# A table gather with a small network behind it: the late tiles' share of the totals goes from SBUF sums to PSUM, and TensorE's order in the last stage changes

## The chip, the core and the metric

One core of a Trainium2 chip. Times are device microseconds of one execution, the median of several runs; lower is better. The engines are TensorE (PE in the profile, its weight loads PEld), VectorE (DVE), ScalarE (ACT), GpSimd (POOL) and SyncE (SP, which here only issues DMAs). SBUF is the working memory, PSUM the memory that TensorE writes, here eight banks of 128 partitions by 512 float32.

## What is computed

For B = 512 samples, 26 tables of 6250 rows by D = 128 and 13 numerical inputs, all float32, the reference computes:

```python
emb = jax.vmap(lambda tab, idx: tab[idx])(tables, cat_features)      # 26 x 512 x 128
emb_btd = jnp.transpose(emb, (1, 0, 2))
wide_num = relu(numerical @ w_wide + b_wide)
cat_sum = jnp.sum(emb_btd, axis=1)                                   # 512 x 128
linear_output = cat_sum + wide_num
x = jnp.concatenate([numerical, emb_btd.reshape(512, 26 * 128)], axis=1)
x = relu(x @ W1 + b1)                                                # 512 x 256
x = relu(x @ W2 + b2)                                                # 512 x 128
dnn_output = x @ W3 + b3                                             # 512 x 1
return sigmoid(dnn_output + linear_output)                           # 512 x 128
```

So every gathered row is used twice: in the first layer, and in the sum over the tables (the total).

## The kernel before

The samples are four chunks of 128 (CH = 4). A tile is the 128 rows of one table for one chunk; a gather brings it with the samples on the partitions, TensorE turns (transposes) it into PSUM, an engine copies it to SBUF, and TensorE multiplies it with that table's slice of W1 into the first layer's four banks. The sums over the tables are held turned, in `emb_sum` in SBUF.

**The body** (L392 to L403) goes through 46 parts of two tiles each (LAST = 46). For each part TensorE turns both tiles (`turn_part`, L336) and multiplies them by W1 (`sum_part`, L353, two products of 256 columns); DVE copies the turned part (L546) and adds it to `emb_sum` (L553). Table 12 is picked by one-hot products instead (L362), with its picture in the two `total` banks, which the body so occupies. Tiles of table 0 of chunks 1 to 3 are fetched row by row with DMAs that ACT and SP issue (L256).

**The last stage** works on the late tables 23 and 24: eight tiles, n = 0 to 7, tile n belonging to chunk n // 2. Each is turned into one of the two `turn` banks (`turn_tile`, L405, L412), copied to `late_t` by ACT (`copy_tile`, L631, L633), multiplied by W1 (`sum_tile`, L415, L421: two products of 128 columns) and, in the kernel before, added from its turned picture to `emb_sum` by DVE (`add_tile`, L580, L587). When a chunk has both tiles, ACT takes the lower half of its first layer through relu (L637) and DVE the upper half (L572); `layer2` (L433, L436) gives the second layer, DVE takes it through relu (`relu_h2`, L575, L577), and `layer3` (L440, L444) adds its product with W3, spread over all 128 columns, to the chunk's total in the bank `total[c % 2]`. Ahead of that `begin_total` (L426, L431) has turned the chunk's `emb_sum` back into that bank by a product with the identity. ACT squashes the total by a sigmoid (`squash`, L640, L642) and SP stores it (L283).

Every product of 128 columns in float32 stands in the profile as two loads and two matmuls, so `sum_tile` and `layer2` are four of each, `begin_total` and `layer3` two, and a turn is one.

The order of each engine's work is written out by hand, and each engine goes through it strictly in that order, waiting on semaphores. TensorE's is in L449 to L468 (printed below). DVE's is in L589 to L598: for each chunk its first add, the upper relu of the chunk before, the second add, and for chunks 1 and 2 the second layer's relu of the chunk before. ACT's is in L647 to L656: copy of the chunk's first tile, lower relu of the chunk before, squash of two chunks before, copy of the second tile. ACT's order is not touched by the change.

In the text behind, turn 4 is `turn_tile(4)`, product 4 is `sum_tile(4)`, and so on, with chunks as well: layer3(0) is the call for chunk 0.

Of the kernel before, what the change touches and what calls it, by code (L numbers as in the profile page):

```python
# [25 lines left out]
def build(nc, num, cat, tables, w_wide, b_wide, W1, b1, W2, b2, W3, b3, out):  # L26
# [58 lines left out]
    with ctx:  # L85
# [6 lines left out]
        def sem(name):  # L92
            return ctx.enter_context(nc.semaphore(name))
# [4 lines left out]
        def late_turn(n):  # L98
            return turn[(LAST + n) % 2][:, 0:P]
# [9 lines left out]
            return first_layer[0][c % 2][:, HW + c // 2 * P:HW + (c // 2 + 1) * P]  # L109

        def total_of(c):
            return total[c % 2][:, 0:D]

        def by_halves(ap):
            return ap.rearrange("x (j q p) -> x q j p", j=HALF, q=2)
# [1 line left out]
        def sum_chunk(c):  # L117
            return emb_sum[:, c % 2, chunk(c // 2)]
# [102 lines left out]
        used = sem("used")  # L221

        late_gathered = [sem(f"late_gathered{n}") for n in range(TILES)]
        late_turned = sem("late_turned")
        late_copied = sem("late_copied")
        late_added = sem("late_added")
# [90 lines left out]
        def _(pe):  # L317
# [35 lines left out]
            def sum_part(i):  # L353
                t, q = PARTS[i]
                wait_w1(t)
                pe.wait_ge(copied, i + 1)
                for k in range(KH):
                    mm = nc.tensor.matmul(first_half(k, q), w1[:, t, chunk(k)], emb_t[:, i % SLOTS, :],  # L358
                                          start=False, stop=False, skip_group_check=True)
                mm.then_inc(used, 1)  # L360
# [44 lines left out]
            def turn_tile(n):  # L405
                c, g = divmod(n, LATE)
                pe.wait_ge(late_gathered[n], 16)
                if n < 2:
                    pe.wait_ge(added, LAST - 1 + n)
                else:  # L410
                    pe.wait_ge(late_added, n - 1)
                nc.tensor.transpose(late_turn(n), emb[:, LATE_TABLES[g], c, :], ident[:, :]  # L412
                                    ).then_inc(late_turned, 1)

            def sum_tile(n):  # L415
                c, g = divmod(n, LATE)
                pe.wait_ge(late_copied, n + 1)
                if c >= 2:
                    pe.wait_ge(h2_ready, c - 1)
                for k, done in enumerate([h1_low_done, h1_high_done]):  # L420
                    mm = nc.tensor.matmul(first_chunk(k, c), w1[:, LATE_TABLES[g], chunk(k)], late_t[:, n, :],  # L421
                                          start=False, stop=False, skip_group_check=True)
                    if g == LATE - 1:
                        mm.then_inc(done, 1)

            def begin_total(c):  # L426

                pe.wait_ge(late_added, (c + 1) * LATE)
                if c >= 2:
                    pe.wait_ge(y_ready, c - 1)  # L430
                nc.tensor.matmul(total_of(c), sum_chunk(c), ident[:, :], start=True, stop=False, skip_group_check=True)  # L431

            def layer2(c):  # L433
                for k, ready in enumerate([h1_low_ready, h1_high_ready]):
# [4 lines left out]

            def layer3(c):  # L440
                pe.wait_ge(h2_ready, c + 1)
                if c == 0:
                    pe.wait_ge(w3_ready, 1)
                nc.tensor.matmul(total_of(c), h2[:, chunk(c)], w3_wide[:, :],  # L444
                                 start=False, stop=True, skip_group_check=True).then_inc(final_done, 1)
# [3 lines left out]
            for c in range(CH):  # L449
                n = c * LATE  # L450
                turn_tile(n)
                if c == 0:
                    sum_part(LAST - 1)
                else:
                    sum_tile(n - 1)
                    begin_total(c - 1)
                if c >= 2:
                    layer3(c - 2)
                turn_tile(n + 1)
                sum_tile(n)  # L460
                if 1 <= c < CH - 1:
                    layer2(c - 1)
            sum_tile(TILES - 1)
            layer2(CH - 2)
            layer2(CH - 1)
            layer3(CH - 2)
            begin_total(CH - 1)
            layer3(CH - 1)  # L468

        @block.vector  # L470
        def _(dve):
# [103 lines left out]
            def relu_h2(c):  # L575
                dve.wait_ge(h2_done, c + 1)
                nc.vector.tensor_scalar(h2[:, chunk(c)], second_chunk(c), b2_col, 0.0, ALU.add, ALU.max  # L577
                                        ).then_inc(h2_ready, 1)

            def add_tile(n):  # L580
                c, g = divmod(n, LATE)
                dve.wait_ge(late_copied, n + 1)
                if n == 0:
                    dve.wait_ge(added, LAST)
                else:
                    dve.wait_ge(late_added, n)
                nc.vector.tensor_tensor(sum_chunk(c), late_turn(n), sum_chunk(c), ALU.add).then_inc(late_added, 1)  # L587

            for c in range(CH):  # L589
                add_tile(c * LATE)  # L590
                if c >= 1:
                    relu_h1_high(c - 1)
                add_tile(c * LATE + 1)
                if 1 <= c < CH - 1:
                    relu_h2(c - 1)
            relu_h1_high(CH - 1)
            relu_h2(CH - 2)
            relu_h2(CH - 1)  # L598

        @block.scalar  # L600
# [79 lines left out]
```

## Time and profile before

| | us |
|---|---|
| median of 3 runs | 236.08 (235.92 to 236.24) |
| time of the profiled execution | 237.66 |
| its span, first to last instruction | 235.9 |
| TensorE busy, matmuls | 126.2 |
| DVE busy | 76.9 |
| ACT busy | 6.2 |
| GpSimd busy | 93.1 |
| mean granted TensorE clock | 0.841 of full |

The profile shows one execution. Its time, 237.66 us, is 1.58 us above the median of the runs beside it, and its span is 0.2 us below that median. Busy times overlap between engines; what counts is who waits for whom at each point. The chain of waits starts from the last instruction and goes back to what released each step. A timeline lists instructions in order of time with start and length; a bracket gives the idle time of that engine just before and what ended it. Lines of like instructions in a row are merged (x4).

### The profile page before, as it was taken

The numbers are of one execution on the slowest core, as the hardware profiler recorded it, in microseconds if no ns is written. First come the engines' busy times: TensorE is split into PE (matmuls) and PEld (weight loads), VectorE is DVE, ScalarE is ACT, GpSimd is POOL, SyncE is SP. The second block draws the span as 40 slices with busy tenths as digits, with TensorE's granted clock in tenths as the row PEclk, the third lists the DMA queues.
The fourth block names the chain that finished last, engine by engine and source line by source line (L and its number), as shares of the span: only waits on it lengthen the run. The fifth ranks groups of instructions, "written<-read, shape, count | busy, mean of one in ns | idle before, by whom it ended". The sixth has DMA issues, their size and how long they took to land.

```text
span 235.9 us, 2252 instructions
## 1 busy us (share of the span) xinstructions
PE 126.2 (54%) x476; PEld 82.6 (35%) x476; DVE 76.9 (33%) x182; ACT 6.2 (3%) x18; POOL 93.1 (39%) x106
## 2 busy tenths in 40 slices
PE   2638200059000700060002719999999999999695
PEld 0415100034000300030002206666666666667594
DVE  3150000033000200110003018677667666845352
ACT  0200000000000000000000000000000000000052
POOL 5777777777777777777771000000000000000000
PEclk9999999999855555575555667999999999999999
DMA  5997613565545443362422003400000000000001
GB/s 150 331 262 170 106 47 51 52 47 103 54 61 45 103 57 48 52 97 54 52 54 63 5 2 93 138 9 4 4 5 4 2 2 1 2 6 2 1 13 34
DMA packets 11244, 14.06 MB, mean 60 GB/s; under 512 B 3308, under 2 KB 8015, under 8 KB 11231
## 3 DMA queue, kind: packets, MB, share of 16 engines
q0 software_dynamic: 3104, 6.36, 20.7%
q1 hardware_dynamic: 4768, 3.80, 5.4%
q10 hardware_dynamic: 3359, 3.76, 5.2%
q8 instruction: 4, 0.07, 0.1%
q14 instruction: 9, 0.07, 0.1%
HBM read 13.65 MB, written 0.26 MB: 59 GB/s over the span
## 4 chain that ended last, share of the span: by engine, by line
SPq 57%; issue 34%; PE 5%; DMA 1%; DVE 1%; ACT 0%; DVEq 0%
SPq L256 50%; SPq L251 7%; PE first_layer L358 1%; PE first_layer L421 1%; DMA first_cat<-in_r_cat_features 1%; PE first_layer L436 1%; PE total L444 1%; DMA emb<-in_L_rec_tables 0%; PE total L431 0%; PE turn L412 0%; PE turn L344 0%; ACT y L642 0%; PE total L320 0%; DVE row_idx L503 0%; DVE cat_row L495 0%
## 5 line engine op out<-in xcount | busy, mean ns | idle before, releaser
L299 POOL DMA_INDIRECT emb<-in_L_rec_tables,row_idx x95 | 89.7, 944 | 29.0 <-issue 29.0
L358 PE MATMUL first_layer<-emb_t,w 128*128 128x256 f32 x184 | 54.4, 423 | 68.2 <-issue 61.3
L358 PEld LDWEIGHTS first_layer<-emb_t,w 128*128 128x128 f32 x184 | 37.6, 212 | 94.4 <-issue 81.8
L369 PE MATMUL total<-hot,block_rows 128*128 128x512 f32 (+1 forms) x98 | 53.8, 656 | 24.8 <-issue 24.8
L546 DVE COPY emb_t<-turn 128x256 f32<-128x256 f32 x46 | 19.4, 422 | 105.4 <-remote 78.3
L526 DVE TENSOR_SCALAR hot<-total,row_no 128x512 f32<-128x512 f32 x49 | 35.3, 742 | 0.0
L369 PEld LDWEIGHTS total<-hot,block_rows 128*128 128x128 f32 (+1 forms) x98 | 17.5, 211 | 32.0 <-issue 32.0
L344 PE MATMUL turn<-ident,emb 128*128 128x128 f32 x92 | 20.3, 304 | 9.0 <-DMA emb<-in_L_rec_tables,row_idx 5.5
L344 PEld LDWEIGHTS turn<-ident,emb 128*128 128x128 f32 x92 | 13.9, 156 | 16.3 <-DMA emb<-in_L_rec_tables,row_idx 6.6
L553 DVE TENSOR_TENSOR emb_sum<-turn,emb_sum 128x256 f32<-128x256 f32 x44 | 18.3, 415 | 0.0
L533 DVE TENSOR_SCALAR wide<-total,b_sb 128x4 f32<-128x4 f32 x1 | 0.2, 222 | 31.6 <-issue 31.6
L633 ACT COPY late_t<-turn 128x128 f32<-128x128 f32 x8 | 2.1, 264 | 219.2 <-PE turn L412 219.2
L421 PE MATMUL first_layer<-late_t,w 128*128 128x128 f32 x32 | 5.0, 280 | 0.1
L421 PEld LDWEIGHTS first_layer<-late_t,w 128*128 128x128 f32 x32 | 4.2, 191 | 0.4 <-ACT late_t L633 0.2
L334 PE MATMUL first_layer<-num_t,w_num 13*128 13x256 f32 x8 | 3.8, 649 | 0.8 <-DVE num_t L509 0.8
L587 DVE TENSOR_TENSOR emb_sum<-turn,emb_sum 128x128 f32<-128x128 f32 x8 | 2.3, 292 | 3.0 <-ACT late_t L633 2.9
L334 PEld LDWEIGHTS first_layer<-num_t,w_num 13*128 13x128 f32 x8 | 2.5, 325 | 1.8 <-DVE num_t L509 1.3
L513 DVE TENSOR_SCALAR pick_lim<-pick_cat 128x512 f32<-128x512 int32 x1 | 0.4, 427 | 7.6 <-DMA pick_cat<-in_r_cat_features 7.6
L320 PE MATMUL total<-ident,cat_row 104*128 104x104 f32 x1 | 0.4, 408 | 4.0 <-DVE cat_row L495 4.0
L436 PE MATMUL first_layer<-h,w 128*128 128x128 f32 x16 | 2.3, 278 | 0.0
L412 PE MATMUL turn<-ident,emb 128*128 128x128 f32 x8 | 2.2, 272 | 0.0
L436 PEld LDWEIGHTS first_layer<-h,w 128*128 128x128 f32 x16 | 2.1, 191 | 0.0
(54 smaller groups left out, 34.2 us busy)
## 6 DMA issues: line engine op xcount, KB each, us to landing
emb<-in_L_rec_tables SPq DMA_DIRECT2D x256, 0.5 KB
block_rows<-in_L_rec_tables ACTq DMA_DIRECT2D x12, 256.0 KB, 2.9
w<-in_L_rec_W SPq DMA_DIRECT2D x2, 1152.0 KB
emb<-in_L_rec_tables ACTq DMA_DIRECT2D x128, 0.5 KB
emb<-in_L_rec_tables,row_idx POOLq DMA_INDIRECT x95
w<-in_L_rec_W SPq DMA_DIRECT2D x1, 768.0 KB
w<-in_L_rec_W SPq DMA_DIRECT2D x1, 256.0 KB
pick_cat<-in_r_cat_features ACTq DMA_DIRECT2D x1, 256.0 KB
```

Source lines behind the costliest of these rows:

```text
L251: eng.load(regs, cat_byte[t * CH + c:t * CH + c + 1, lo:lo + REGS])
L256: eng.dma_start(emb[b:b + 1, t, c, :].bitcast(U8), row_bytes[t:t + 1, bass.ds(at, ROW)]).then_inc(fetched[t, c], 16)
L299: nc.gpsimd.indirect_dma_start(emb[:, t, c, :], None, rows, bass.IndirectOffsetOnAxis(ap=index, axis=0)).then_inc(landed, 16)
L334: nc.tensor.matmul(first_half(k, q), w1_num[:, chunk(k)], cols, start=True, stop=True)
L344: mm = nc.tensor.transpose(turn[i % 2][:, chunk(j)], emb[:, t, c, :], ident[:, :])
L358: mm = nc.tensor.matmul(first_half(k, q), w1[:, t, chunk(k)], emb_t[:, i % SLOTS, :], start=False, stop=False, skip_group_check=True)
L369: mm = nc.tensor.matmul(pick_bank[:, :], block_rows[0:n, j, :], hot[0:n, j % PICK_RING, :], start=(j == 0), stop=(j == PER))
L421: mm = nc.tensor.matmul(first_chunk(k, c), w1[:, LATE_TABLES[g], chunk(k)], late_t[:, n, :], start=False, stop=False, skip_group_check=True)
L436: mm = nc.tensor.matmul(second_chunk(c), w2[:, k, :], h1[:, k, chunk(c)], start=False, stop=False, skip_group_check=True)
L526: nc.vector.tensor_scalar(hot[:, j % PICK_RING, :], pick_row[:, :], row_no[:, j:j + 1], None, ALU.is_equal).then_inc(hot_ready, 1)
L546: nc.vector.tensor_copy(emb_t[:, i % SLOTS, :], turn[i % 2][:, 0:HW]).then_inc(copied, 1)
L553: nc.vector.tensor_tensor(emb_sum[:, q, :], turn[i % 2][:, 0:HW], emb_sum[:, q, :], ALU.add).then_inc(added, 1)
```

## The change

- `total_of(c)`: the four totals get places of their own, two in each `total` bank, where before chunks c and c + 2 shared the first 128 columns of one bank.
- `begin_totals` replaces the four calls of `begin_total`: the `emb_sum` of all four chunks, as the body leaves them, are turned into the totals one after the other, right behind the last part's products.
- `add_tile` on DVE takes the gathered tile as it lies in SBUF, not its turned picture, and adds it to the total in PSUM. It waits for `begin_totals`, for its gather, for the add before, and for chunks 2 and 3 for the squash of the chunk that shares the bank. It no longer waits for ACT's copy.
- `turn_tile` waits for ACT's copy out of the `turn` bank instead of DVE's add; `layer3` waits for the chunk's adds.
- TensorE's order: from chunk 1 on the products of the previous chunk's second tile and of this chunk's first come together, ahead of this chunk's second turn; `layer3(c - 2)` stands right behind the chunk's first turn; `layer2(CH - 2)` comes ahead of the last product.
- DVE's order: the upper relu ahead of both adds, the second layer's relu behind them, for all chunks.

```diff
--- before.py
+++ after.py
@@ -109,7 +109,7 @@
             return first_layer[0][c % 2][:, HW + c // 2 * P:HW + (c // 2 + 1) * P]
 
         def total_of(c):
-            return total[c % 2][:, 0:D]
+            return total[c % 2][:, c // 2 * D:(c // 2 + 1) * D]
 
         def by_halves(ap):
             return ap.rearrange("x (j q p) -> x q j p", j=HALF, q=2)
@@ -221,6 +221,7 @@
         used = sem("used")
 
         late_gathered = [sem(f"late_gathered{n}") for n in range(TILES)]
+        totals_begun = sem("totals_begun")
         late_turned = sem("late_turned")
         late_copied = sem("late_copied")
         late_added = sem("late_added")
@@ -408,7 +409,7 @@
                 if n < 2:
                     pe.wait_ge(added, LAST - 1 + n)
                 else:
-                    pe.wait_ge(late_added, n - 1)
+                    pe.wait_ge(late_copied, n - 1)
                 nc.tensor.transpose(late_turn(n), emb[:, LATE_TABLES[g], c, :], ident[:, :]
                                     ).then_inc(late_turned, 1)
 
@@ -423,12 +424,14 @@
                     if g == LATE - 1:
                         mm.then_inc(done, 1)
 
-            def begin_total(c):
-
-                pe.wait_ge(late_added, (c + 1) * LATE)
-                if c >= 2:
-                    pe.wait_ge(y_ready, c - 1)
-                nc.tensor.matmul(total_of(c), sum_chunk(c), ident[:, :], start=True, stop=False, skip_group_check=True)
+            def begin_totals():
+
+
+                pe.wait_ge(added, LAST)
+                for c in range(CH):
+                    mm = nc.tensor.matmul(total_of(c), sum_chunk(c), ident[:, :], start=(c < 2), stop=False,
+                                          skip_group_check=True)
+                mm.then_inc(totals_begun, 1)
 
             def layer2(c):
                 for k, ready in enumerate([h1_low_ready, h1_high_ready]):
@@ -439,6 +442,7 @@
 
             def layer3(c):
                 pe.wait_ge(h2_ready, c + 1)
+                pe.wait_ge(late_added, (c + 1) * LATE)
                 if c == 0:
                     pe.wait_ge(w3_ready, 1)
                 nc.tensor.matmul(total_of(c), h2[:, chunk(c)], w3_wide[:, :],
@@ -451,20 +455,18 @@
                 turn_tile(n)
                 if c == 0:
                     sum_part(LAST - 1)
+                    begin_totals()
                 else:
+                    if c >= 2:
+                        layer3(c - 2)
                     sum_tile(n - 1)
-                    begin_total(c - 1)
-                if c >= 2:
-                    layer3(c - 2)
+                sum_tile(n)
                 turn_tile(n + 1)
-                sum_tile(n)
-                if 1 <= c < CH - 1:
+                if c >= 1:
                     layer2(c - 1)
             sum_tile(TILES - 1)
-            layer2(CH - 2)
             layer2(CH - 1)
             layer3(CH - 2)
-            begin_total(CH - 1)
             layer3(CH - 1)
 
         @block.vector
@@ -578,23 +580,25 @@
                                         ).then_inc(h2_ready, 1)
 
             def add_tile(n):
+
                 c, g = divmod(n, LATE)
-                dve.wait_ge(late_copied, n + 1)
-                if n == 0:
-                    dve.wait_ge(added, LAST)
-                else:
+                dve.wait_ge(totals_begun, 1)
+                if c >= 2:
+                    dve.wait_ge(y_ready, c - 1)
+                if n > 0:
                     dve.wait_ge(late_added, n)
-                nc.vector.tensor_tensor(sum_chunk(c), late_turn(n), sum_chunk(c), ALU.add).then_inc(late_added, 1)
+                dve.wait_ge(late_gathered[n], 16)
+                nc.vector.tensor_tensor(total_of(c), total_of(c), emb[:, LATE_TABLES[g], c, :], ALU.add
+                                        ).then_inc(late_added, 1)
 
             for c in range(CH):
-                add_tile(c * LATE)
                 if c >= 1:
                     relu_h1_high(c - 1)
+                add_tile(c * LATE)
                 add_tile(c * LATE + 1)
-                if 1 <= c < CH - 1:
+                if c >= 1:
                     relu_h2(c - 1)
             relu_h1_high(CH - 1)
-            relu_h2(CH - 2)
             relu_h2(CH - 1)
 
         @block.scalar
```

## Rows read from the trace of the kernel before

**Rows 1.** The page: shares of the span on the chain that ended last, by engine.

```profile
SPq 57%; issue 34%; PE 5%; DMA 1%; DVE 1%; ACT 0%; DVEq 0%
```

**Rows 2.** Windows: from:to, length, busy (x instructions) per engine, granted clock, DMA share, GB/s.

```profile
218.00:220.40 2.40, 0.00 (x0) 0.00 (x0) 0.00 (x0) 0.00 (x0) 0.00 (x0) 1.00 0.01 2
223.45:230.55 7.10, 7.10 (x60) 6.83 (x58) 3.85 (x13) 3.43 (x13) 0.00 (x0) 1.00 0.04 11
```

**Rows 3.** Timeline, TensorE's weight loads: start, us, engine, line, operation, count [idle <-releaser].

```profile
220.47 0.14 PEld L344 LDWEIGHTS turn<-ident,emb 128*128 128x128 f32 x1 [2.85 <-DMA emb<-in_L_rec_tables]
...
223.67 0.73 PEld L358 LDWEIGHTS first_layer<-emb_t,w 128*128 128x128 f32 x4
224.65 0.53 PEld L421 LDWEIGHTS first_layer<-late_t,w 128*128 128x128 f32 x4
```

**Rows 4.** The same timeline, from layer2(1) to the last turn.

```profile
228.49 0.53 PEld L436 LDWEIGHTS first_layer<-h,w 128*128 128x128 f32 x4
228.94 0.14 PEld L412 LDWEIGHTS turn<-ident,emb 128*128 128x128 f32 x1
229.05 0.53 PEld L421 LDWEIGHTS first_layer<-late_t,w 128*128 128x128 f32 x4
229.50 0.30 PEld L431 LDWEIGHTS total<-ident,emb_sum 128*128 128x128 f32 x2
229.72 0.30 PEld L444 LDWEIGHTS total<-w_wide,h 128*128 128x128 f32 x2
229.94 0.14 PEld L412 LDWEIGHTS turn<-ident,emb 128*128 128x128 f32 x1
```

**Rows 5.** The same timeline, from the last product to the last instruction.

```profile
230.83 0.52 PEld L421 LDWEIGHTS first_layer<-late_t,w 128*128 128x128 f32 x4 [0.25 <-ACT late_t L633]
231.27 1.03 PEld L436 LDWEIGHTS first_layer<-h,w 128*128 128x128 f32 x8
232.43 0.30 PEld L444 LDWEIGHTS total<-w_wide,h 128*128 128x128 f32 x2
232.65 0.30 PEld L431 LDWEIGHTS total<-ident,emb_sum 128*128 128x128 f32 x2
232.93 0.30 PEld L444 LDWEIGHTS total<-w_wide,h 128*128 128x128 f32 x2
```

**Rows 6.** Timeline of ACT in the last stage.

```profile
229.36 0.27 ACT L633 COPY late_t<-turn 128x128 f32<-128x128 f32 x1 [0.59 <-PE turn L412]
229.58 0.37 ACT L637 ACTIVATE h<-first_layer,vec_cols 128x128 f32<-128x128 f32 x1
230.25 0.37 ACT L642 ACTIVATE y<-total,wide 128x128 f32<-128x128 f32 x1 [0.30 <-PE total L444]
230.52 0.26 ACT L633 COPY late_t<-turn 128x128 f32<-128x128 f32 x1
...
232.96 0.87 ACT L642 ACTIVATE y<-total,wide 128x128 f32<-128x128 f32 x2 [1.24 <-PE total L444]
```

**Rows 7.** Timeline of DVE in the last stage.

```profile
229.25 0.35 DVE L577 TENSOR_SCALAR h<-first_layer,vec_cols 128x128 f32<-128x128 f32 x1 [0.16 <-PE first_layer L436]
229.66 0.29 DVE L587 TENSOR_TENSOR emb_sum<-turn,emb_sum 128x128 f32<-128x128 f32 x1
229.87 0.34 DVE L572 TENSOR_SCALAR h<-first_layer,vec_cols 128x128 f32<-128x128 f32 x1
...
231.58 0.35 DVE L572 TENSOR_SCALAR h<-first_layer,vec_cols 128x128 f32<-128x128 f32 x1 [0.48 <-PE first_layer L421]
232.03 0.85 DVE L577 TENSOR_SCALAR h<-first_layer,vec_cols 128x128 f32<-128x128 f32 x2
```

**Rows 8.** Timeline of DVE near the start, two dependent operations, the second writing PSUM.

```profile
14.65 0.43 DVE L516 TENSOR_SCALAR pick_neg<-pick_lim 128x512 f32<-128x512 f32 x1
15.11 0.70 DVE L519 TENSOR_TENSOR total<-pick_neg,pick_lim 128x512 f32<-128x512 f32 x1
```

**Rows 9.** Timeline of TensorE's weight loads in the body, at granted clock 0.50.

```profile
77.42 1.35 PEld L358 LDWEIGHTS first_layer<-emb_t,w 128*128 128x128 f32 x4 [19.55 <-issue]
```

## Prediction

> **What bounds the kernel now.** I read the chain of waits first. Most of it is SP's queue [rows 1]: the row-by-row fetches, whose last landing releases TensorE at 220.47 after an idle stretch [rows 3]. The change touches nothing ahead of that, nor the body's last parts behind it, so a gain or loss can only arise from 223.5 us on. For that stretch I read the windows and then the timelines. In the windows the reader is to see that TensorE has no idle time between 223.45 and 230.55 (7.10 busy of 7.10), while DVE is busy for 3.85 and ACT for 3.43, and that the clock is full [rows 2]. TensorE's throughput is the limit there. The engines beside it have slack, but their hand-overs don't hurt only because the order of TensorE's work puts enough between a producer and its user. From 230.83 on it is otherwise: TensorE waits for other engines, and a chain of latencies leads to the end [rows 5].
>
> **The prices.** I count in slots, the starts of the weight loads. Product or layer2: 228.49 to 228.94, 0.45. Turn: 0.11. begin_total or layer3: 0.22 [rows 4]. Hand-overs, from a load's start:
> - Turn to product by ACT's copy: load 228.94 [rows 4], copy 229.36 for 0.27 [rows 6]; the copy of 230.52 ends at 230.78 and the product starts at 230.83 [rows 5, 6], 0.05 on. Sum 0.74.
> - layer2 to layer3 by DVE's relu: load 228.49 [rows 4], relu 229.25 for 0.35 [rows 7]; the relu of 232.03 ends at 232.38 and layer3 starts at 232.43 [rows 5, 7]. Sum 0.76 + 0.35 + 0.05 = 1.16.
> - Product to layer2's upper half: load 230.83, relu 231.58 for 0.35, again 0.05: 1.15 [rows 5, 7].
> - Product to ACT's lower relu: 229.05 to 229.58, 0.53. layer3 to squash: 229.72 to 230.25, 0.53 [rows 4, 6]. ACT's next operation starts 0.27 after a squash has started (230.25, 230.52), DVE's 0.21 after an add (229.66, 229.87) [rows 6, 7].
>
> **The parts of the change.**
>
> *The begins.* Same four, same 0.22 each. Three lay between other TensorE work and one, begin_total(3), between layer3(2) and layer3(3): 232.65 to 232.87 [rows 5]. There it filled a hole: the relu that layer3(3) needs ends at 0.85 after 232.03, that is 232.88, and layer3(3) starts at 232.93 [rows 5, 7]. Taking it away from the end gains nothing, and putting it at the start costs its 0.22 in a stretch where TensorE is full.
>
> *layer2(2) ahead of the last product.* It stood behind it, beside the wait for the relus of chunk 3, which is idle time otherwise. Moving it delays the last product by 0.45, less the wait that it covers.
>
> *The copy and the turns.* The last body products start at 223.67 and product 0 at 224.65, with one turn before it [rows 3], so the begins start at 224.54 and last 0.89, to 225.43. Product 0 then runs to 225.87 and turns 1 and 2 take until 226.09. Product 1 comes next, but its copy needs 225.87 + 0.74 = 226.61. **First stall: 0.52.** Before, product 0 stood between turn 1 and turn 2.
>
> *layer3 behind the turn.* Products 1 and 2 go to 227.50, turn 3 to 227.61, layer2(0) starts at 227.61 (its upper half, from 227.83, has its relu since 226.61 + 1.15 = 227.76) and ends at 228.05. Turn 4 ends at 228.16, and layer3(0) follows at once, though its relu needs 227.61 + 1.16 = 228.77. **Second stall: 0.61.** Behind the waiting layer3 stand products 3 and 4, which need nothing of it. Before, a product and a begin (0.67) stood here [rows 4]; they hid exactly this. Chunk 3 repeats it: products 3 and 4 from 228.99, turn 5 at 229.88, layer2(1) at 229.99, turn 6 from 230.43 to 230.54, layer3(1) at 229.99 + 1.16 = 231.15. **Third stall: 0.61.**
>
> *The adds, and DVE's new wait.* Eight adds read SBUF instead of a turned picture and write PSUM. No row shows that form: 0.29 for the old form [rows 7] is one bound, 0.70 for an add of four times the columns that writes PSUM [rows 8] the other; nothing excludes slightly less than 0.29, which would change nothing. I take 0.29, since the size is the same and the 0.70 is for 512 columns. Adds 0 to 3 lie in DVE's idle time. Add 4 waits for squash(0), and the relu of chunk 1's second layer is queued behind it; layer3(1) waits for that. squash(0) follows the lower relu of chunk 1: 228.99 + 0.53 = 229.52, squash from 229.79 to 230.16. With the 0.03 between dependent operations (14.65 + 0.43 to 15.11) [rows 8], adds 4 and 5 start at 230.19 and 230.51, and DVE can start the relu 0.21 later, at 230.72. It is due at 229.99 + 0.76 = 230.75. So the detour by the squash just fits, cost 0; at 0.70 an add it would cost 0.8. ACT has no queue ahead of any copy that counts.
>
> *The end.* layer3(1) at 231.15, products 5 and 6 to 232.26, turn 7 to 232.37, layer2(2) to 232.82, and product 7 at 232.26 + 0.74 = 233.00. **Fourth stall: 0.18.** From the last product to layer3(3) it was 232.93 - 230.83 = 2.10 [rows 5], all by hand-overs: 1.15 to layer2(3)'s upper half, a relu, layer3. Nothing in that is changed, and squash and store behind it are as before.
>
> **The sum.** The last product moves from 230.83 to 233.00: **+2.17**. As a check by parts: work moved ahead of it, 0.22 + 0.45 = 0.67; new stalls 0.52 + 0.61 + 0.61 + 0.18 = 1.92; less the 0.34 that it waited before (turn 7 at 229.94, two steps of 0.11 and 0.45 to 230.50, start at 230.83 [rows 4, 5]) and some 0.06 lost around turn 2. That is 2.19, the same within rounding. The profiled span would be 235.9 + 2.2 = 238.1, its time 237.66 + 2.17 = 239.8. The median lies 1.58 below the profiled time, and I carry that over: 236.08 + 2.17 = 238.25, say **238.2**.
>
> A rule that speaks for smaller stalls: by the Trainium skill (TensorE: Matmul & The Clock Gate, Part 2, Step-by-step) TensorE can pull weight loads ahead of matmuls in flight, though matmuls keep their order. By it one load (two that overlap take 0.30 [rows 5], so under 0.2) might be done within each wait and the four stalls would shrink to a sum of about 1.2, for some 237.5. The trace speaks against it for this wait: the load of product 7 began only at 230.83, after the copy [rows 5], though W1 had long been there.
>
> **Rivals.**
> - *Only throughput counts.* If the hand-overs were met (an order of waits that I misread, or relus and copies that come sooner once DVE no longer waits for the copy), only the 0.67 moved ahead of the last product remains, less the 0.34 + 0.06 of old waits: +0.27, 236.35. For it speaks that TensorE was full for 7.1 us without one wait [rows 2]. Against it: a turn and its product now stand 0.11 apart, where the row has 0.74. This is the case that is not slower.
> - *A gain.* If begin_total(3) were on the path at the end rather than in a hole, and the hand-overs met, the 0.22 comes off: 235.86. Against it stand the 232.88 and 232.93 above. A gain of over 0.2% needs twice that, from something that I don't see.
> - *DVE becomes the bound.* With an add of 0.70, from any price above about 0.32 on, the squash, add, add, relu detour decides chunk 3: layer3(1) 0.8 later; then adds 6 and 7 and a relu (some 1.8) stand in front of the upper relu of chunk 3, from squash(1) on, and cost about another 0.8. Total +3.8, 239.9.
> - *The clock falls in the gaps.* TensorE would have three gaps of over 0.5 us in 7. At the lower clock four loads of 256-column products took 1.35 [rows 9] against 0.73 [rows 3]. Some 25 slots behind the third stall would then cost up to 0.11 more each, but half lie beside waits: +1.4 more, 239.6. Against it: the 2.40 us without any work at 218 left the clock at full [rows 2]. The Trainium skill (TensorE: Matmul & The Clock Gate, Part 1: The HAM clock gate) has it that an idle TensorE is put back to half its clock; the trace agrees for much longer gaps only.
>
> **How the numbers follow.** Forecast with stalls at row prices: 0.82. Only throughput: 0.06. A gain or no change by something unseen: 0.04. DVE as the bound: 0.05. Clock: 0.03. The forecast's own range: each of the four stalls can be off by 0.15 either way if hand-overs vary, the adds can cost up to 0.4 before they reach the rival, and the runs before spread by 0.3: 237.5 to 238.9. With the other cases left out that holds about 8 in 10. A measurement of this kernel can tell 0.2%, 0.47 us, from no change. Faster: 0.03. Within 0.2%: 0.07, the throughput case and part of the unseen. Slower: 0.90.
>
> **What would show it.** In TensorE's timeline behind the begins: idle time before product 1 ended by ACT's copy, before layer3(0) and layer3(1) by DVE's relu L577, about 0.5 to 0.6 each, and a small one before product 7. The begins 0.89 in a row without idle time. DVE's add 0.29. The last product to the last layer3 2.10 as before. TensorE idle for less than 1 us between 223.5 and the last product would prove the throughput case; layer3(1) released by a relu that itself stood behind an add, the DVE case. The prediction is wrong as a whole if the body itself ends at another time than 223.5.

## The result and the profile after

The changed kernel takes 239.03 us in the median of 5 runs (238.05 to 239.89) against 236.08 (235.84 to 236.35) before: slower, ratio 1.0119, 95% interval 1.0087 to 1.0151. A second comparison gave a ratio of 1.0107 (1.0084 to 1.0129), 238.58 against 236.43. The forecast was 238.2, with a range of 237.5 to 238.9: the 239.03 lies 0.13 us above that range, the 238.58 in it.

| | before, first profile | after, first profile |
|---|---|---|
| span | 235.9 | 237.2 |
| last fetched row releases TensorE | 220.47 | 219.49 |
| turn 0 | 223.45 | 222.48 |
| last product (product 7) | 230.83 | 232.20 |
| layer3(3) | 232.93 | 234.30 |
| turn 0 to last product | 7.38 | 9.72 |
| last product to layer3(3) | 2.10 | 2.10 |

All starts are those of the weight loads. The late stage, counted from turn 0 so that the body's end doesn't matter, grew by 2.34 us. The last fetched row happened to release TensorE 0.98 earlier in this profile than in that of before, and the body ended as much earlier.

TensorE's weight loads of the changed kernel, from turn 0 on (start, us, line, operation, count, idle time before and what ended it), beside [rows 3 to 5]:

```profile
222.48 0.14 PEld L413 LDWEIGHTS turn<-ident,emb 128*128 128x128 f32 x1
222.69 0.73 PEld L359 LDWEIGHTS first_layer<-emb_t,w 128*128 128x128 f32 x4
223.45 1.08 PEld L432 LDWEIGHTS total<-ident,emb_sum 128*128 128x128 f32 x8
224.45 0.53 PEld L422 LDWEIGHTS first_layer<-late_t,w 128*128 128x128 f32 x4
224.89 0.25 PEld L413 LDWEIGHTS turn<-ident,emb 128*128 128x128 f32 x2
225.63 0.97 PEld L422 LDWEIGHTS first_layer<-late_t,w 128*128 128x128 f32 x8 [0.48 <-ACT late_t L637]
...
227.78 0.30 PEld L448 LDWEIGHTS total<-w_wide,h 128*128 128x128 f32 x2 [0.57 <-DVE h L579]
...
230.35 0.30 PEld L448 LDWEIGHTS total<-w_wide,h 128*128 128x128 f32 x2 [0.76 <-DVE h L579]
...
231.57 0.53 PEld L439 LDWEIGHTS first_layer<-h,w 128*128 128x128 f32 x4
232.20 0.52 PEld L422 LDWEIGHTS first_layer<-late_t,w 128*128 128x128 f32 x4
```

The reader is to see three brackets where [rows 4] has none: TensorE waits for ACT's copy before product 1, and for DVE's relu before each of the first two layer3. (The idle time of the loads is counted from the end of the last one, so a stall in slots, the starts of the loads, is a little longer: 0.52, 0.60 and 0.79.) The fourth stall has no bracket: layer2(2) starts at 231.57 and would end at 232.02, and product 7 starts 0.18 later.

The same stretch as a window (from:to, length, busy time of each engine, granted clock):

```profile
222.48:232.20 9.72, 8.62 (x66) 7.63 (x65) 3.96 (x13) 3.64 (x13) 0.00 (x0) 1.00 0.03 8
```

TensorE had no idle time at all in [rows 2] (and 0.06 us up to the last product); now it has 1.10 us of it, and the clock stays full. The four stalls add up to 2.09 us in slots, since the matmuls of the loads before a stall still run into it.

### The profile page after: what moved, and what is told of

Read it like the earlier page. It is cut to its first block, busy times and chain, and to the rows that moved or that the text cites. A ratio compares the mean times of both kernels' runs of the same rounds, so it can differ in the third digit from the quotient of the medians.

```text
span 237.2 us, 2257 instructions
## 1 busy us (share of the span) xinstructions
PE 125.3 (53%) x476; PEld 81.7 (34%) x476; DVE 77.2 (33%) x182; ACT 6.2 (3%) x18; POOL 93.0 (39%) x106
## 4 chain that ended last, share of the span: by engine, by line
SPq 59%; issue 33%; PE 5%; ACT 1%; DVE 1%; DMA 1%; DVEq 0%
SPq L257 51%; SPq L252 7%; PE first_layer L359 1%; PE first_layer L422 1%; SPq L270 1%; PE first_layer L439 1%; PE total L448 1%; DMA emb<-in_L_rec_tables 1%; DVE h L579 0%; PE total L432 0%; PE turn L345 0%; ACT h L641 0%; ACT y L646 0%; DVE total L591 0%; PE turn L413 0%
## 5 line engine op out<-in xcount | busy, mean ns | idle before, releaser
L370 PE MATMUL total<-hot,block_rows 128*128 128x512 f32 (+1 forms) x98 | 53.2, 649 | 27.4 <-issue 27.4
L345 PE MATMUL turn<-ident,emb 128*128 128x128 f32 x92 | 20.0, 301 | 8.0 <-DMA emb<-in_L_rec_tables,row_idx 6.2
L591 DVE TENSOR_TENSOR total<-total,emb 128x128 f32<-128x128 f32 x8 | 2.4, 298 | 2.8 <-PE total L432 2.0
L448 PE MATMUL total<-w_wide,h 128*128 128x128 f32 x8 | 1.9, 313 | 1.1 <-DVE h L579 1.1
L574 DVE TENSOR_SCALAR h<-first_layer,vec_cols 128x128 f32<-128x128 f32 x4 | 1.4, 350 | 3.1 <-PE first_layer L422 3.0
```

The costliest lines, as they stand in the source:

```text
L345: mm = nc.tensor.transpose(turn[i % 2][:, chunk(j)], emb[:, t, c, :], ident[:, :])
L370: mm = nc.tensor.matmul(pick_bank[:, :], block_rows[0:n, j, :], hot[0:n, j % PICK_RING, :], start=(j == 0), stop=(j == PER))
```

## The experiments

Two things were in question: which part of the change costs, TensorE's order or the new totals; and why the medians differ by more than the 2.34 us of the late stage. Late stage below means turn 0 to the last product; where an expectation counts from the turn that the last row releases, it is 2.98 us more while the clock stays full.

### The two kernels again

> The kernel before, once more. The late stretch, from the turn that the last fetched row releases to the last product's first load, should be 10.4 us as in its first profile, whatever the body does. Theory 1 (what the late stage doesn't explain of the 2.95 us between the medians, some 0.6 us, is the body ending at a varying time): the moment at which the last row releases TensorE differs by some tenths up to 1.5 us from profile to profile of the same kernel. Theory 2 (the change moves the body): that moment is within 0.2 us in all profiles of the kernel before, and later in all of the changed one.

> The changed kernel, once more. The late stretch should be 12.7 us as in its first profile. Theory 1 (the body's end varies by itself): the ratio to the kernel before comes nearer to 1.010, the 2.35 us of the late stretch alone. Theory 2 (the change moves the body): the ratio stays near 1.0119.

The kernel before had 236.05 us beside 236.43 for the same code (ratio 0.9999, 0.9973 to 1.0025), the changed one the 1.0107 told above. Two weight loads of the kernel before in this profile, the turn released by the last row and the last product:

```profile
219.15 0.14 PEld L344 LDWEIGHTS turn<-ident,emb 128*128 128x128 f32 x1 [0.90 <-DMA emb<-in_L_rec_tables]
...
229.51 0.52 PEld L421 LDWEIGHTS first_layer<-late_t,w 128*128 128x128 f32 x4 [0.25 <-ACT late_t L633]
```

From one to the other it is 10.36 us, as in the first profile (220.47 to 230.83); the changed kernel again had 12.71 (218.86 to 231.57). The late stage repeats to 0.01 us. The moment at which the last row releases TensorE does not: 220.47, 219.15 and, in a third profile below, 220.39 with the old code; 219.49 and 218.86 with the new; 219.32 to 220.48 in four variants below that leave the body alone. So nothing shows the change moving the body later, and its own cost is 2.35 us, 1.0100, which lies in both intervals. The medians differ by 2.95 us in the first comparison and by 2.15 in the second, once above and once below that. The variation of the body is large enough for both; which executions had it was not traced.

### The new totals alone, and the new order alone

The changed kernel with the old order of TensorE's calls:

```diff
                 if c == 0:
                     sum_part(LAST - 1)
                     begin_totals()
                 else:
-                    if c >= 2:
-                        layer3(c - 2)
                     sum_tile(n - 1)
-                sum_tile(n)
+                if c >= 2:
+                    layer3(c - 2)
                 turn_tile(n + 1)
-                if c >= 1:
+                sum_tile(n)
+                if 1 <= c < CH - 1:
                     layer2(c - 1)
             sum_tile(TILES - 1)
+            layer2(CH - 2)
             layer2(CH - 1)
```

> Begins in front and DVE's adds to the totals as in the changed kernel, but TensorE's order of turns, products, layer2 and layer3 as before. Theory (the order costs): the stall before product 1 shrinks to 0.1 and those before layer3 to 0.16 and 0.3; the last product comes 0.55 us later than before, late stretch 10.9 us, time about 236.7. Rival (the early begins and the adds with their wait for the squash cost): late stretch over 12.3 us, time about 238.5.

The late stage took 8.06 us (222.31 to 230.37), 0.69 more than before and 1.67 less than the changed kernel: near the theory, far from the rival. Yet the time was 237.46, ratio 1.0045 (1.0029 to 1.0061), because something that I had not expected was late next. TensorE's load of layer2(3)'s upper half, then DVE's timeline:

```profile
230.37 0.52 PEld L422 LDWEIGHTS first_layer<-late_t,w 128*128 128x128 f32 x4 [0.25 <-ACT late_t L638]
...
232.23 0.30 PEld L439 LDWEIGHTS first_layer<-h,w 128*128 128x128 f32 x2 [0.62 <-DVE h L575]
```

```profile
231.57 0.35 DVE L580 TENSOR_SCALAR h<-first_layer,vec_cols 128x128 f32<-128x128 f32 x1 [0.52 <-PE first_layer L439]
231.84 0.34 DVE L575 TENSOR_SCALAR h<-first_layer,vec_cols 128x128 f32<-128x128 f32 x1
```

With layer2(2) back behind the last product, DVE's new order has chunk 2's second relu (231.57) in front of chunk 3's upper relu. The latter was due at 230.37 + 0.75 = 231.12 and started at 231.84; the end grew from 2.10 to 2.80 us. The two halves of the change were made for each other: DVE's order needs layer2(2) ahead of the last product.

The kernel before with the new order of TensorE's calls, its begins put behind the chunk's products:

```diff
                 if c == 0:
                     sum_part(LAST - 1)
                 else:
+                    if c >= 2:
+                        layer3(c - 2)
                     sum_tile(n - 1)
+                sum_tile(n)
+                if c >= 1:
                     begin_total(c - 1)
-                if c >= 2:
-                    layer3(c - 2)
                 turn_tile(n + 1)
-                sum_tile(n)
-                if 1 <= c < CH - 1:
+                if c >= 1:
                     layer2(c - 1)
             sum_tile(TILES - 1)
-            layer2(CH - 2)
             layer2(CH - 1)
```

> The kernel before with the changed TensorE order alone: both products ahead of a chunk's second turn, layer3 right behind the first turn, layer2(2) ahead of the last product; sums, begins (now behind the chunk's products) and adds as before. Theory (the order costs): stalls of 0.5 before product 1, 0.6 before layer3(0) and layer3(1), 0.2 before product 7; late stretch 12.3 us, time about 238.1. Rival (the new totals cost): late stretch at most 10.8 us, time about 236.3.

```profile
224.57 0.97 PEld L421 LDWEIGHTS first_layer<-late_t,w 128*128 128x128 f32 x8 [0.48 <-ACT late_t L633]
...
227.01 0.30 PEld L444 LDWEIGHTS total<-w_wide,h 128*128 128x128 f32 x2 [0.62 <-DVE h L577]
...
229.66 0.30 PEld L444 LDWEIGHTS total<-w_wide,h 128*128 128x128 f32 x2 [0.62 <-DVE h L577]
...
231.73 0.52 PEld L421 LDWEIGHTS first_layer<-late_t,w 128*128 128x128 f32 x4
```

These weight loads show the changed kernel's stalls in the old data path. The late stage was 9.42 us, the time 238.69, ratio 1.0105 (1.0084 to 1.0126), which can't be told from the changed kernel's 238.58. Order alone costs 2.05 us of late stage, the new totals alone 0.69 with a late end; the change 2.35. With the new order in place, the new totals add only 0.30: 0.22 for the begin that came from the end, and 0.08 at the two layer3, whose stalls in slots are 0.66 and 0.65 here and 0.60 and 0.79 in the changed kernel. The order is the cause of most of it.

### The stalls one by one

The next four ran on a chip that gives the kernel before 133.95 us, of which below. Their late stages are read in the same way and set beside the 9.72 us of the changed kernel, which was not itself profiled on that chip. What supports it is that the stalls which an experiment leaves alone are as long there (before product 1 an idle time of 0.48, before layer3(0) 0.57).

```diff
                     relu_h1_high(c - 1)
+                if c == 2:
+                    relu_h2(c - 1)
                 add_tile(c * LATE)
                 add_tile(c * LATE + 1)
-                if c >= 1:
+                if c >= 1 and c != 2:
                     relu_h2(c - 1)
```

> The changed kernel with one step of DVE's order moved: the second layer's relu of chunk 1 goes ahead of adds 4 and 5. Theory (layer3(1)'s stall of 0.79 is 0.61 of plain hand-over and 0.18 of the detour squash, add, add): that stall falls to 0.6, the others stay, late stretch 12.5 us instead of 12.7. Rival (0.79 is the hand-over itself, longer in the second layer3 than in the first for another reason): late stretch unchanged at 12.7.

```profile
126.56 0.30 PEld L448 LDWEIGHTS total<-w_wide,h 128*128 128x128 f32 x2 [0.57 <-DVE h L579]
```

The second layer3 now waits as long as the first (0.57 idle instead of 0.76), late stage 9.53 instead of 9.72: theory. The plain hand-over is 0.6, the detour by the squash 0.19.

```diff
-                sum_tile(n)
-                turn_tile(n + 1)
+                if c == 0:
+                    turn_tile(n + 1)
+                    sum_tile(n)
+                else:
+                    sum_tile(n)
+                    turn_tile(n + 1)
```

> The changed kernel with turn 1 ahead of product 0 instead of behind it. Theory (product 1's stall of 0.5 is the missing distance between turn and product): the stall falls to 0.1, late stretch 12.3 us, time 0.4 us less than the changed kernel's. Rival (the gap only moves on, since layer3(0) waits for a relu whose time is set elsewhere): late stretch 12.6 to 12.7.

```profile
121.35 0.14 PEld L413 LDWEIGHTS turn<-ident,emb 128*128 128x128 f32 x1
121.53 1.08 PEld L422 LDWEIGHTS first_layer<-late_t,w 128*128 128x128 f32 x8
```

Product 1 starts 0.18 behind turn 2's start, 0.07 of it stall. Late stage 9.39, a gain of 0.33 where 0.4 was expected: the eight loads take 1.08 instead of 0.97, since product 2 follows its own turn too closely as well and waits 0.1 for its copy.

```diff
                 else:
+                    sum_tile(n - 1)
                     if c >= 2:
                         layer3(c - 2)
-                    sum_tile(n - 1)
                 sum_tile(n)
```

> The changed kernel with layer3(c - 2) behind the first product of a chunk instead of ahead of it. Theory (the two stalls before layer3 come from nothing being left between layer2 and layer3): they fall from 0.60 and 0.79 to 0.16 and 0.3, and the last product comes 0.9 us earlier, late stretch 11.8 us, time about 237.6. Rival (DVE, with its adds behind the squash, sets the pace of a chunk, so that TensorE's order doesn't matter): the second stall stays above 0.7 and the late stretch above 12.3.

```profile
125.97 0.30 PEld L448 LDWEIGHTS total<-w_wide,h 128*128 128x128 f32 x2 [0.17 <-DVE h L579]
...
127.37 0.52 PEld L422 LDWEIGHTS first_layer<-late_t,w 128*128 128x128 f32 x4
```

The long waits are gone, only 0.17 idle is left at layer3(1); late stage 8.80 us, 0.92 less than the changed kernel, as worked out. Moving layer3 past one product gives back 0.9 of the 2.35 us. Its ratio to the kernel before there was 1.0048 (1.0026 to 1.0070), against 1.0093, 1.0080 and 1.0100 for the other three on this chip.

```diff
                 dve.wait_ge(totals_begun, 1)
-                if c >= 2:
-                    dve.wait_ge(y_ready, c - 1)
-                if n > 0:
-                    dve.wait_ge(late_added, n)
                 dve.wait_ge(late_gathered[n], 16)
+                if c >= 2 and n % LATE == 0:
+                    dve.wait_ge(late_added, n)
+                    dve.wait_ge(y_ready, c - 1)
+                elif n > 0:
+                    dve.wait_ge(late_added, n)
```

> The changed kernel with the order of the adds' waits changed alone: those long satisfied (the gather, the begins) first, the one that is released last (the squash for adds 4 and 6, the add before for the others) last. Theory (each wait that stands behind the last released one costs DVE's queue 0.05 to 0.1 us on the chain, twice behind the squash and the first add): add 5 starts 0.35 after add 4 instead of 0.50, layer3(1)'s stall falls from 0.79 to about 0.63, late stretch 12.55. Rival (the 0.50 is the latency of one add to a dependent one in PSUM): nothing changes, 12.7.

First the chain of waits of the changed kernel between squash(0) and layer3(1), in order of time; then that of this experiment, from the same squash to add 5:

```profile
228.90 0.27 ACT y L646
229.17 0.03 DVEq L590
229.20 0.05 issue
229.25 0.31 DVE total L591
229.56 0.03 issue
229.59 0.02 DVEq L589
229.61 0.05 issue
229.66 0.05 DVEq L590
229.71 0.04 issue
229.75 0.30 DVE total L591
230.05 0.26 DVE h L579
```

```profile
125.45 0.03 issue
125.48 0.05 DVEq L589
125.53 0.04 issue
125.58 0.31 DVE total L592
125.89 0.03 issue
125.91 0.05 DVEq L591
125.96 0.04 issue
126.01 0.30 DVE total L592
```

The expectation was missed: late stage 9.70, a gain of 0.02. Add 5 does start sooner behind add 4 (0.43 instead of 0.50), so the 0.50 is not the latency of an add in PSUM. But the edit also took the wait for the squash out of add 5, which leaves it three waits instead of four, and the number may count more than the order: in the changed kernel's first profile add 1, with three waits in the old order, followed add 0 by 0.39 (224.76, 225.15). The two were not tested apart. And add 4 now starts 0.14 behind the squash's end instead of 0.08, and the gain is gone. From the squash's end it is 0.03 and 0.05 to the add in the one, 0.03, 0.05 and 0.04 in the other; why the second takes longer was not found.

### The new totals at their best

The first experiment's order of TensorE, with DVE's mended:

```diff
                     relu_h1_high(c - 1)
+                if c == 2:
+                    relu_h2(c - 1)
                 add_tile(c * LATE)
                 add_tile(c * LATE + 1)
-                if c >= 1:
+                if c == 1:
                     relu_h2(c - 1)
             relu_h1_high(CH - 1)
+            relu_h2(CH - 2)
```

> The begins in front and the adds to the totals kept, in the best order I know for them: TensorE's turns, products and layers as in the kernel before, the relu of chunk 1's second layer ahead of adds 4 and 5, the upper relu of chunk 3 ahead of the second layer's relu of chunk 2. Theory (the new totals save nothing, since the adds and the last begin lay in slack, and cost 0.2 at the start and some waits at layer3): turn 0 to the last product 7.95 us, the end 2.1 again, 0.6 us slower than before on a chip at 236 us. Rival (the new totals are worth something once the order is mended): under 7.4 us, no slower than before.

```profile
230.68 0.52 PEld L422 LDWEIGHTS first_layer<-late_t,w 128*128 128x128 f32 x4 [0.23 <-ACT late_t L641]
...
232.78 0.30 PEld L448 LDWEIGHTS total<-w_wide,h 128*128 128x128 f32 x2 [0.20 <-DVE h L580]
```

Turn 0 was at 222.77, so the late stage is 7.91 us and the end 2.10: 0.53 more than before in all. The time, 237.07 against 236.81, ratio 1.0006 (0.9984 to 1.0027), can't tell that from nothing; its interval reaches 0.64 us. What the trace does tell is that the new totals, freed of the changed order, bring no gain in the best order that I know for them.

### The kernel before again, and two that beat it

> The kernel before, a third time. Two chips so far gave it 236 and 134 us, with the same instructions. Theory: on the chip at 134 us the gathers, one each 1.25 us to about 124.6, come so late that turns of the late stage wait for them, so that from turn 0 to the last product it takes about 8.5 us instead of 7.4 and the changed order has less to lose (0.6 to 1.4 us instead of 2.4). On a chip at 236 us: 7.4 us again, all gathers landed at 140. Rival: 7.4 us on both kinds of chip.

This run was on a chip at 236 us, so the expectation's first half was not put to the test; the late stage was 7.37 us once more. But this profile (237.5 us of span) shows one thing that makes the body's end vary. The window and the weight loads behind the wait for the last row:

```profile
220.40:224.00 3.60, 3.60 (x11) 2.90 (x12) 1.51 (x4) 0.00 (x0) 0.00 (x0) 0.55 0.00 0
```

```profile
220.39 0.14 PEld L344 LDWEIGHTS turn<-ident,emb 128*128 128x128 f32 x1 [2.34 <-DMA emb<-in_L_rec_tables]
220.40 1.18 PEld L358 LDWEIGHTS first_layer<-emb_t,w 128*128 128x128 f32 x4
...
225.06 0.14 PEld L412 LDWEIGHTS turn<-ident,emb 128*128 128x128 f32 x1
```

Behind an idle stretch of 2.34 us the granted clock was near half for 3.6 us, and from the released turn to turn 0 it took 4.67 us instead of 2.98. With 239.26 us this execution was the slowest of its 14.

The kernel before with turn 7 and product 6 ahead of layer3(1), and ACT's copy of tile 7 ahead of the squash of chunk 1:

```diff
-                if c >= 2:
+                if c == 2:
                     layer3(c - 2)
                 turn_tile(n + 1)
                 sum_tile(n)
+                if c == 3:
+                    layer3(c - 2)
...
-                if c >= 2:
+                if c == 2:
                     squash(c - 2)
                 copy_tile(c * LATE + 1)
             relu_h1_low(CH - 1)
+            squash(CH - 3)
```

> The kernel before with one thing mended: turn 7 and product 6 ahead of layer3(1), and ACT's copy of tile 7 ahead of the squash of chunk 1, which goes behind the lower relu of chunk 3. Theory: product 7 no longer waits 0.33 for a copy that stood behind a squash; turn 0 to the last product falls from 7.38 to 7.05 us, the end behind it stays 2.10, time 0.3 us less on a chip at 236 us; on one at 134 us nothing, since the last gather decides. Rival (turn to product is too short even so): a wait of 0.2 to 0.3 before product 7 stays.

```profile
231.90 0.30 PEld L444 LDWEIGHTS total<-w_wide,h 128*128 128x128 f32 x2
232.12 0.53 PEld L421 LDWEIGHTS first_layer<-late_t,w 128*128 128x128 f32 x4
```

No wait is left before product 7; from turn 0 at 225.08 it is 7.04 us, as expected. Time 236.30 against 236.81, ratio 0.9970 (0.9952 to 0.9989), in which the 0.33 us of the late stage lies.

With it, the part that waits for SP's rows made the body's last:

```diff
-    PARTS += [(t, q) for t in OTHERS[-4:-1] for q in range(2)] + [(0, 1)]
-    PARTS += [(t, q) for t in OTHERS[-1:] for q in range(2)]
+    PARTS += [(t, q) for t in OTHERS[-4:] for q in range(2)] + [(0, 1)]
```

> The last one with the part that waits for SP's row-by-row fetch (tiles 1 and 3 of table 0) made the body's last instead of the third from the end. Theory (on a chip at 236 us TensorE idles 0.9 to 2.5 us for that fetch with two parts of work, 2.2 us, behind it): the idle time falls to under 0.4, time 1 to 2 us less than before, about 234.8. On a chip at 134 us the fetch is done in time and nothing changes. Rival: SP's queue is no bound, another wait takes the place of the idle time, time as in the run beside it.

```profile
219.25 0.36 PEld L343 LDWEIGHTS turn<-ident,emb 128*128 128x128 f32 x2
219.57 0.73 PEld L357 LDWEIGHTS first_layer<-emb_t,w 128*128 128x128 f32 x4
220.33 0.36 PEld L343 LDWEIGHTS turn<-ident,emb 128*128 128x128 f32 x2
220.66 0.73 PEld L357 LDWEIGHTS first_layer<-emb_t,w 128*128 128x128 f32 x4
221.42 0.14 PEld L411 LDWEIGHTS turn<-ident,emb 128*128 128x128 f32 x1
```

The turns at 220.33 are those of the fetched rows, now without any wait; turn 0 is at 221.42, the last product at 228.46. The time is 234.58 us (234.34 to 235.31) against 236.81, ratio 0.9904 (0.9881 to 0.9927): faster than the kernel before and so than the changed one, which did not run on this chip. It was not run on a chip at 134 us.

## Why the prediction was right, and where it was off

**What bounds.** Right: the change touched the late stage alone, and there TensorE was full before and isn't now.

**The begins.** Right. They took from 223.45 to 224.45 (1.00, not 0.89, but they began 0.11 sooner behind the body's products), product 0 started 1.76 behind the last body products, as worked out, and the one taken from the end gained nothing: the end stayed 2.10, and it was 2.10 too in the experiment with the old totals, which kept that begin.

**The four stalls.** In slots, forecast and measured: product 1, 0.52 and 0.52; layer3(0), 0.61 and 0.60; layer3(1), 0.61 and 0.79; product 7, 0.18 and 0.18. The mechanism of the first three was shown by taking each away: turn 1 ahead of product 0, layer3 behind a product. The fourth was in the trace as worked out, but was not tested by itself.

**The adds.** The step that failed is "the detour by the squash just fits, cost 0". The adds themselves were priced right (0.30, so writing PSUM costs nothing over the 0.29 of [rows 7]). But I took 0.03 between dependent operations from [rows 8], a pair with a single wait between them; adds 4 and 5 have four waits each, and on the chain they took 0.08 behind the squash and 0.20 between the adds. So the second layer's relu of chunk 1 started at 229.96, 0.95 behind layer2(1), instead of 0.76. The detour cost 0.19, as the experiment with the relu ahead of the adds measured. The rival in which DVE is the bound so came true in its first place, by the sign that I had given for it (a relu that itself stood behind an add), at 0.19 and not 0.8. Its second place did not: the upper relu of chunk 3 started at 232.95, 0.75 behind the product, on time. By the sum of the prediction itself the detour starts to cost from an add of about 0.305, not 0.32, so there was less room than I said.

**The sum.** 2.17 forecast, 2.34 measured in the late stage, the difference being that detour. By parts it is 0.67 of work moved ahead, 2.09 of stalls, less the 0.40 of old waits (0.33 and not 0.34 at product 7): 2.36. On the 236.43 of the second comparison 2.34 gives 238.8, and 238.6 was measured.

**The 0.6 us above that in the first comparison.** I took the body to end at the same time with both kernels, and said that the prediction would be wrong as a whole if it did not. That was too strict. The last row released TensorE at 220.47 in the profile of before and at 219.15 in another of the same code, and the 1.58 us between the profiled execution and the median is of that size. The difference of the late stages was sound; the level of a single execution says little. The variation took the 239.03 of the first comparison out of the range; and that the medians of the second differ by 2.15 us, as good as the forecast 2.17, is luck, since the late stage alone costs 2.35.

**The rivals.** Only throughput counts fell, by 1.10 us of idle time where there had been none. My sign for it, less than 1 us of idle time, was set too near: I counted stalls in slots, and half of them showed as idle time of the matmuls. The gain fell with it. The clock rival, though, was closer than I held it to be. I argued that 2.40 us without work had left the clock at full. In two later profiles (the kernel before at 220.39 and the one with the last copy first, at 220.48) idle stretches of 2.34 and 2.51 us were followed by a clock near half, 0.55 and 0.53; in the first profile of before 2.85 were not, nor 2.35 in that of the new totals in the better order. The gaps of 0.5 to 0.8 us of the changed order never did it: its late stage ran at 1.00 in both profiles. The Trainium skill (TensorE: Matmul & The Clock Gate, Part 1: The HAM clock gate) has an idle TensorE put back to half its clock, and has the moment at which the clock changes differ from run to run. The traces agree with the fall and with its varying; that so short a stretch is enough is what these runs show.

**The rule on early weight loads.** The Trainium skill (TensorE: Matmul & The Clock Gate, Part 2, Step-by-step) lets loads be pulled ahead of matmuls in flight. At all four stalls the load itself began only when the wait was over (225.63, 227.78, 230.35, 232.20), though for the products its weights, a slice of W1, had long been there. The full stalls were paid, and the 237.5 worked out by that rule did not come.

**What stays open.** Why one chip runs the same instructions in 134 us was not found. SP's 256 row fetches, 7.14 to 219.47 in the first profile of before, were done there by 113.4, and the mean clock of every run there was 0.99 to 1.00. On it the four kernels were 0.6 to 1.4 us slower than before, some 0.8 to 1.0 less than their late stages are longer than 7.37; the kernel before was not profiled there. An estimate: its turn 7 would be due 6.49 behind turn 0, at about 125.2, and the gathers are issued there until 124.6 and take 3.3 in the median to land, so its late stage is likely longer than 7.37. That was not shown.

## What to carry to other kernels

Where one engine is full and its neighbours half idle, the order of its work is what pays for the hand-overs: before moving a call, write down for each producer and consumer the hand-over time (here 0.74 by ACT's copy, 1.16 by the second layer's relu, both from the producer's start), the producer's own slot (0.11 and 0.45) and the work left between them (0.11 and 0.11 after the change). The hand-over less the other two is the stall: 0.52 and 0.60. Moving work off an engine's neighbours or off the end gains nothing where it filled a hole, and a new wait in a strict queue can delay everything behind it. The idle time worth filling was elsewhere: a part waiting for a late transfer, with ready work queued behind it, gave some 0.7% by changing places (0.9904 against 0.9970 without it).

## What the runs showed of the hardware that I had not expected

- The clock fell to near half (0.55, 0.53) behind idle stretches of 2.34 and 2.51 us with full work on both sides, and stayed full in other profiles behind 2.35 and 2.85; where it fell it cost 1.6 to 1.7 us.
- From the end of the operation that an add waits for to the start of that add it took 0.08 to 0.14 us (229.17 to 229.25, 125.44 to 125.58), and between two dependent adds 0.09 and 0.12 where the second has three waits (225.06 to 225.15, 125.89 to 126.01), 0.20 where it has four (229.56 to 229.75).
- An add of 128 by 128 elements with one input in PSUM takes 0.30 us with its output in PSUM, against 0.29 with its output in SBUF.
- The same kernel took 134 us on one chip and 236 to 237 on the others that it ran on.
